# Loading attention rows in 32-row transfers, quarter by quarter from two queues, with a new merge order

## The chip, the cores and the metric

One core of a Trainium2 chip runs the whole program. The metric is the device time of one execution in microseconds (us); lower is better. The engines named here are TensorE (PE, with its weight loads PEld), VectorE (DVE), ScalarE (ACT), GpSimd (POOL) and SyncE (SP), which here only issues transfers. A transfer (DMA) is issued by SP or by ACT, in the order of that engine's own instructions, and is carried out by the core's 16 DMA engines.

## The reference

The input x has 8 batches of 512 tokens with 128 features. Stage A is a global attention, stage B two layers of a windowed attention with a gated MLP.

```python
h = layernorm(x) * (1 + ca) + sa
q = (h @ Wq + bq).reshape(b, 16, 8, 512)     # k, v alike: a reshape, no transpose
attn = softmax(einsum('bhdt,bhds->bhts', k, v) * temperature)
x = x + ga * einsum('bhdt,bhts->bhds', q, attn).reshape(b, t, d)
h = layernorm(x) * (1 + cb) + sb
y = h
for l in range(2):                            # windows of 64, 8 heads of 64
    y = layer(y)                              # shift, qkv, norms, rotary, attention, gated MLP
x = x + gb * y
```

The reshape matters here: one attention head is made of whole tokens. A head's 8 rows of 512 numbers are the 32 tokens' features laid end to end, so k and v have to be laid out anew, by way of DRAM, before the scores can be computed.

## The kernel before

**Stage A** works on one batch at a time, batches 0 to 7. k and v are each split into a high part and a low part (`hi`, `lo`), written to the DRAM scratch tensors `k_scr` and `v_scr` by four transfers each (`a_parts`, or `values_first` on ACT for batch 0), and read back as rows into `k_rows` and `v_rows`. The scratch has the shape (q, hh, 4, 8, 512), with head = 4q + hh. For one hh, "a quarter" below, the rows are 4 heads (q = 0 to 3) of 32 rows with 512 numbers: 128 partitions of 2 KB, 256 KB in all. `rows_in` reads such a quarter in the pieces that `PIECES` lists: for hh = 0 one transfer of 4 heads, for hh = 1 one of 3 heads and one of 1, for hh = 2 two of 2, for hh = 3 one of 1 and one of 3; seven transfers for k and seven for v. `v_rows` has two slots, `k_rows` one. SP issues all the v quarters of a batch (`a_values_in`), then the k quarters one by one (`a_keys_in`), where quarter hh of batch b waits until batch b-1 has finished its maxima for it. Only batch 0 is different: its k quarters come from SP and its v quarters from ACT (`values_first_in`), ahead of ACT's first work of the merged streams.

A batch has 32 steps n, 8 for each quarter. Step n is a pair of score matmuls on 32 partitions (`a_scores`, L436), a row maximum on DVE (L1151), two exponentials on ACT (L866); every second step the weights are normed by a reciprocal (L1155) and a product on POOL (L764), and the values are summed by 4 matmuls (`a_values`, L445) into one bank over the whole batch. The scores of a quarter wait for its v rows and k rows (`rows_landed`). At its end, DVE multiplies the sum by a gate (L1162) and POOL adds it to x (L753).

**Stage B** works in two streams, x with batches 0, 1, 2, 4, 6 and y with 3, 5, 7. Stream x starts while stage A is running; stream y has buffers that stage A also uses and begins when all of A is over. A batch of B enters with a layer norm (`b_enter_var`, `b_enter_normalize`), a transposition (L487) and a modulation on ACT (L921), and then has per layer 12 projections (L494), 8 transpositions (L501), windowed attention (L512 to L540), the output product (L550), the MLP (L569, L575), and at its end a transposition (`b_leave`) and two DVE operations (`b_out`, L1282 and L1286).

**The order** in which an engine takes steps of the three streams is written out by hand in `ORDER`: one letter for each step of stage A (`a`), stream x and stream y. Each engine has its own string and works through it in that order; semaphores hold it up where data isn't there. `BANKS` names the PSUM bank of every matmul step of PE's string. PE's string has 1166 letters, and both versions of a string have equally many of each letter, but for SP's.

Of the kernel before, what the change touches and what calls it, by code (L numbers as in the profile page):

```python
# [48 lines left out]
PIECES = [[(q, n, (q + hh) % HQ) for q, n in ((0, HQ - hh), (HQ - hh, hh)) if n] for hh in range(HQ)]  # L49
# [29 lines left out]
    ),
    "DVE": (  # L80
        "aaaaaaaaaaaaaaaaaaaaaaaaaaaaaaaaaaaaaaaaaaaaaaaaaaaaaaaaaaaaaaaaaaxaaaaaxaaaaaaaaaxaaaaaaaaaaxxaaaxx"
        "aaxxaxxaaxxaxaaxaaaaaaaaaaxaaaaaaaaaaaaxxaaxaaaaaaaaaaaaxxxaaaxaaxxxxaxaaaxxaaxxxaaaxxaaaaaaaxaaaxax"
        "aaaaxaxaaaaaaxaxaxaaaxxaaaaaxaaaxaaaxaxaaxaxaxaxxaaxaxaxaaaaaaaaaaaxaaaaxxaxxxxaaaxaaxxaaxxxaaaaxxxx"
        "axaaxaaxaaxaaxaxaaaaaaaxaxaaaaaaxxxaaaaxaaaaaaxaxaaaxaaaaaaxaaaaxaxxaxaaaxxxaaxxaaaxxaxaaaaaaaaaxaaa"
        "aaaaaaaaaaxxaxxxxaaaxxxaxxxaaaaaxxxxaxaaxaaaxaaxaaaaxaxaaaxaaaxaaaaaxxxaaaaxaxaaaxaaxaxaaxxaxxaaxxaa"
        "axaxxaaaaaaaaxaaaaaaxxxxaxxaxaaaaaxxxxxaaaxxaxxxaaaxaaaxaaaxaaxaxaaaxaxaaaaaaaxxxaaaxaaaaaaxxaxayxyx"
        "xxyxxxxxxxyxyxyyyyxyxxyxxyxxxyyyxxxxxxxxxxyxxyyxyyyyyxxyxyyyxyyyyyyyxxxxxyxyxyyyxyxxxxxyyxyxyxyxyyyx"
        "yxyxyxxxxyyxxxyyxyxxxyxxxxxxyyyxyyyyyxxyxyyyxyyyxxxyyyxyxxyyxyyxyxyxxxxxxxxyyyxyxyxyyxyxxxxyxxyxyxyx"
        "xxxyyyyxxxyyxyxxyxyyyxyyyyyxxyxyyyxyyyyyyxxxyxxyxyxyyyxyxxxxxyyxxyxyxyyyyxyxxyyxxxxyyxxxyyxxxyxxyxxx"
        "xxyyyxyyyyyxxyxyyyxyyyxxxyyyxyxxyyxyyxyxxxyxxxxxyyxxyxyxyyyxyxxxxxxyxyxxyxxxyxxyxxxyxyyyxxyyxyxxxyyy"  # L90
        "yyyyxxxyyyxxyyyyyyyyxyxxyxyxxyyyxyxxxxyyxyyyyxyyyyxxyxxxxyyxyyxxxxyxyxxxxxyxxyyxyyyyyxxyyyyyyxyyyyxy"
        "yyyyxxyxyxxyyyyy"
    ),
    "ACT": (
        "aaaaaaaaaaaaaaaaaaaaaaaaaaaaaaaaaaaaaaaaaaaaaaaaxaaaaaaaaxaaaaxaaaaxxxxaxxxxaaxxaxxaxaaxaxxxxaxaaaxx"
        "xaaaaaaaaaaaxxaaaaaaaaaxaaxxxaxxxaaaxxxaxxaxaaaxaaaaxaaaaxxaaaxaaaaaxaaaxaxxaxaxaxxxaxxaxaxaxaaxxxxa"
        "aaaxaaxxxaxaaaxxaaxxxaxaxaxxxaaaaxxxxaaaxxaaaxaaaaaxaxaaaxaaaaaaaaxaaaxxaaaaxxaxxxxxxaxxaxaxaaxaaaxx"
        "xaxxaaaaxxaxxaaaaaaaaxxaxaaxxxxxaxaxaaxxxaxaxxaaaaaxaaaaxaaaxaaxaaaxaxaxxxxaxaxxxaxxaxaxaaaxxxxxaaxa"
        "aaxxaaxaaxxxxxaaaxaxxxaaxxaxxaaxaxxaaaaxaaaxaxaaaxaaaaaaaxxxyxxxxxxyxyxxxxxyyyxyyyxxxxxyyyxxyxyxyxxy"
        "xxxxyyyxxyyxxyxyxxxyyxxyyyyxyyyyxyyxyyyxyxyyxxxyxxxyxxxyxxyxxyxxxxyyxyyxxxyyyxyyxxyyxxxxyxyxyyxxxyxy"  # L100
        "yxxyyyxyxyyyyxyyyxyyyxyxyyyyyxxyxxyxxxxxxxyxxxxyxxxxxxyxxxxyyxyxyyxyyxxxyyyxxyyxyxyyxxxyyyyxyxyyyyxy"
        "yyyxyyyxyyyxyxyyyxyyxxxyxxxyxxxyxxyxxxxxyxxyyxxyyyxxyyyyxxyyxxxxyxyxxyyyyxyxxyxxyyxyxyyyyxyyyyxyyxyx"
        "yyyyyxxyxxyxxxxxxxxyxxyxxxxxxxxxyxxyyxxyxyyxyxyxxyxyxxyxxyxxyyyxxyyyyxyyyyxyyxyyxyyyyyxyyyyxxyyxxyxx"
        "yyxxxyxxxyyxyxxxxxyxxxyyxyyyyyyyyxxyyxxxyxxxyyyyxyxxxyyxyxyxxyyyyyyyyxyyyyxyyxyyxyyyy"
    ),
# [1314 lines left out]
```

## Time and profile before

| | us |
|---|---|
| median of three runs | 1280.28 (1274.93 to 1286.37) |
| the profiled execution's own time | 1273.49 |
| its span, from the first to the last instruction | 1271.4 |
| PE busy / DVE busy / ACT busy / POOL busy in the span | 1046.8 / 946.8 / 922.3 / 504.1 |

The profiled execution is faster than the median run by 6.8 us. A row of the trace has a start, a duration, the engine, the line of the kernel, the operation and its tensors, and how often it came; in brackets how long the engine stood idle before it and what ended that. `SPq` and `ACTq` are these engines' issuing of transfers, and their durations are those of the issuing instructions, not of the transfers.

### The profile page before, as it was taken

Reading aid. Unit: us, or ns where it says so; the run is one execution under the profiler, and the core shown is the slowest. Engines: PE = TensorE matmul, PEld = TensorE weight load, DVE = VectorE, ACT = ScalarE, POOL = GpSimd, SP = SyncE. Lnnn points to the kernel's source line nnn. Section 1 sums busy time; section 2 is a strip of 40 time slices with the busy share of each in tenths; the row PEclk is TensorE's granted clock in tenths of the full one; section 3 lists DMA queues with packets and bytes.
Section 4 is the critical chain, followed back from the end, with each engine's and each line's share of the span. In section 5 each row is a group of like instructions: output and inputs, shape, how many; then the busy total and the mean of one; then the engine's idle time right before and its main releaser. Section 6 shows DMA issues by size and latency. Waiting matters only on the chain.

```text
span 1271.4 us, 23838 instructions
## 1 busy us (share of the span) xinstructions
PE 1046.8 (82%) x8124; PEld 524.9 (41%) x8124; DVE 946.8 (74%) x1945; ACT 922.3 (73%) x2782; POOL 504.1 (40%) x577
## 2 busy tenths in 40 slices
PE   2678888798888878988877898888898888898888
PEld 2232234333432334334324644644553553554463
DVE  2669977888779868776789578578758769758854
ACT  1688789788978897879855866756666765875673
POOL 4011523134312621343028437516735725645740
PEclk8687889897888888968888999999899999998999
DMA  6331213022021140210001101101100200110110
GB/s 209 138 132 36 101 43 106 28 67 82 16 97 45 34 117 13 88 58 19 1 9 30 31 1 30 31 10 38 30 2 1 47 23 9 31 30 1 31 31 17
DMA packets 24647, 59.15 MB, mean 47 GB/s; under 512 B 2832, under 2 KB 3024, under 8 KB 23376
## 3 DMA queue, kind: packets, MB, share of 16 engines
q1 hardware_dynamic: 23394, 55.53, 14.6%
q10 hardware_dynamic: 1134, 2.10, 0.5%
q8 instruction: 67, 1.10, 0.4%
q14 instruction: 52, 0.43, 0.1%
HBM read 23.98 MB, written 18.87 MB: 34 GB/s over the span
## 4 chain that ended last, share of the span: by engine, by line
PE 41%; DVE 30%; ACT 14%; issue 6%; POOL 4%; DMA 3%; SPq 1%; ACTq 0%; DVEq 0%; POOLq 0%
DVE neg_max L1151 8%; PE psum L494 6%; PE psum L445 5%; ACT E L866 5%; PE psum L550 4%; PE psum L569 4%; PE psum L436 4%; PE psum L540 4%; ACT rot_work L960 4%; DVE rot_work L1218 3%; DVE work L1214 3%; DVE ss L1222 3%; PE psum L575 3%; PE psum L529 2%; PE psum L519 2%
## 5 line engine op out<-in xcount | busy, mean ns | idle before, releaser
L866 ACT ACTIVATE E<-psum,neg_max 128x512 f32<-128x512 f32 x512 | 347.3, 704 | 85.0 <-DVE neg_max L1151 63.1
L1151 DVE TENSOR_REDUCE neg_max<-psum 128x2 f32<-128x1024 f32 x256 | 308.2, 1214 | 80.3 <-PE psum L436 78.0
L786 POOL TENSOR_TENSOR work<-work,rot_work 128x512 f32<-128x512 f32 x128 | 162.7, 1272 | 159.5 <-DVE rot_work L1218 159.2
L436 PE MATMUL psum<-v_rows,k_rows 32*128 32x512 f32 x512 | 135.0, 554 | 96.2 <-ACT E L866 56.7
L799 POOL TENSOR_TENSOR rot_work<-rot_work,rz 128x512 f32<-128x512 f32 x128 | 132.7, 1042 | 183.5 <-DVE rz L1245 183.4
L960 ACT ACTIVATE rot_work<-psum,neg 128x128 f32<-128x128 f32 x512 | 182.8, 394 | 29.9 <-DVE neg L1240 16.0
L494 PE MATMUL psum<-wqkv_sb,hs 128*128 128x512 f32 x384 | 188.7, 620 | 9.6 <-DVE hs L1208 4.3
L445 PE MATMUL psum<-E,qz 128*32 128x512 f32 x1024 | 160.8, 705 | 2.5 <-POOL qz L764 2.5
L764 POOL TENSOR_TENSOR qz<-qT,rz 128x32 f32<-128x32 f32 x128 | 31.0, 242 | 329.7 <-DVE rz L1155 317.1
L436 PEld LDWEIGHTS psum<-v_rows,k_rows 32*128 32x128 f32 x512 | 53.0, 205 | 247.9 <-issue 133.0
L794 POOL TENSOR_TENSOR work<-work,rn 128x512 f32<-128x512 f32 x128 | 133.0, 1052 | 28.7 <-DVE rn L1110 28.4
L960 ACT ACTIVATION_READ_ACCUMULATOR rot_work<-psum,neg 128x1 f32 x512 | 119.1, 233 | 0.0
L501 PE MATMUL psum<-ident,work 128*128 128x128 f32 x512 | 88.1, 307 | 33.4 <-POOL work L794 29.9
L866 ACT ACTIVATION_READ_ACCUMULATOR E<-psum,neg_max 128x1 f32 x512 | 113.2, 221 | 0.0
L932 ACT ACTIVATE rot_work<-psum 128x512 f32<-128x512 f32 x128 | 76.9, 605 | 46.7 <-DVE ss L1222 24.1
L1240 DVE TENSOR_REDUCE neg<-psum 128x4 f32<-128x512 f32 x128 | 85.4, 677 | 30.6 <-PE psum L519 30.3
L529 PE MATMUL psum<-ident,rot_work 128*128 128x128 f32 x512 | 83.6, 291 | 28.3 <-POOL rot_work L799 21.9
L494 PEld LDWEIGHTS psum<-wqkv_sb,hs 128*128 128x128 f32 x384 | 65.3, 191 | 91.6 <-issue 50.6
L569 PE MATMUL psum<-work,w_sb 128*128 128x512 f32 (+1 forms) x192 | 95.7, 634 | 5.2 <-ACT work L975 4.0
L1214 DVE TENSOR_TENSOR work<-psum,rot 128x512 f32<-128x512 f32 x128 | 87.0, 679 | 17.2 <-ACT rot_work L932 16.1
L970 ACT ACTIVATE prT<-psum 128x512 f32<-128x512 f32 x128 | 78.4, 620 | 25.0 <-PE psum L540 16.7
L501 PEld LDWEIGHTS psum<-ident,work 128*128 128x128 f32 x512 | 62.7, 155 | 71.5 <-POOL work L794 54.5
(121 smaller groups left out, 1679.3 us busy)
## 6 DMA issues: line engine op xcount, KB each, us to landing
work<-v_al SPq DMA_DIRECT2D x16, 512.0 KB, 4.4
work<-v_al SPq DMA_DIRECT2D x16, 384.0 KB, 6.2
k_scr<-hi SPq DMA_DIRECT2D x16, 256.0 KB, 3.0
k_scr<-lo SPq DMA_DIRECT2D x16, 256.0 KB, 3.4
v_scr<-hi SPq DMA_DIRECT2D x14, 256.0 KB, 3.1
v_scr<-lo SPq DMA_DIRECT2D x14, 256.0 KB, 3.4
k_rows<-k_scr SPq DMA_DIRECT2D x16, 192.0 KB
v_rows<-v_scr SPq DMA_DIRECT2D x14, 192.0 KB
```

The lines of the kernel that those rows point to most:

```text
L436: pe.matmul(bank, k_rows[r:r + 32, hh, P * j:P * (j + 1)], v_rows[r:r + 32, b % 2, hh, :], start=True, stop=True).then_inc(full, 1)
L445: last = pe.matmul(O_BANK[32 * q:32 * q + 32, :], qz[:, hh, j % QZ_SLOTS, q, :], E[:, (b * NG + g) % E_RING, q, :], start=(g == 0), stop=( ...
L494: pe.matmul(bank, hs[s][:, P * i:P * (i + 1)], wqkv_sb[:, l, INNER * c:INNER * (c + 1)], start=True, stop=True).then_inc(full, 1)
L501: last = pe.transpose(bank[:, P * p:P * (p + 1)], qk[s][:, i, w, P * p:P * (p + 1)], ident[:])
L569: pe.matmul(bank[0:CH[c]], w1_sb[:, l, o:o + CH[c]], h2T[s], start=True, stop=True).then_inc(full, 1)
L786: pool.tensor_tensor(qk[s][:, i, w, :], qk[s][:, i, w, :], sinp[s][:, n % 2, :], ALU.add).then_inc(rot_sum[s], 1)
L794: pool.tensor_tensor(v, v, rn[s][:, i, w, :].unsqueeze(2).broadcast_to([P, H, DH]), ALU.mult).then_inc((q_ready, k_ready)[w][s], 1)
L799: pool.tensor_tensor(pr[s][:, u % PR_SLOTS], pr[s][:, u % PR_SLOTS], rz2[s][:, u, :].unsqueeze(2).broadcast_to([P, 4, 2 * W]), ALU.mult).t ...
L866: act.activation(E[:, (b * NG + g) % E_RING, 2 * half + m, :], pair[:, m], ACT.Exp, bias=neg_max[:, n, m:m + 1], accum_out=z[:, n, m:m + 1 ...
L960: last = act.activation(pr[s][:, u % PR_SLOTS, w, :], bank[:, 2 * W * w:2 * W * (w + 1)], ACT.Exp, bias=neg2[s][:, u, w:w + 1], accum_out= ...
L1151: dve.tensor_reduce(neg_max[:, n, :], pair, AX.X, ALU.max, negate=True).then_inc(max_ready, 1)
L1214: dve.tensor_tensor(qk[s][:, i, w, :].rearrange("p (h d) -> p h d", h=H), bank.rearrange("p (h d) -> p h d", h=H), rot[:, l, i, w, 0, :].u ...
```

## The change

`PIECES` is gone. `rows_in` now issues four transfers of 32 rows (64 KB) for each quarter, one per head, to the same places as before. For k and v together a batch has 32 row transfers instead of 14. In batch 0, ACT issues only the v rows of quarter 0; SP issues the k rows of quarter 0, then v and k of quarter 1, of 2 and of 3. In the later batches SP still issues all v quarters ahead of the k quarters, but each v quarter is a step of its own in the merge order.

```diff
-PIECES = [[(q, n, (q + hh) % HQ) for q, n in ((0, HQ - hh), (HQ - hh, hh)) if n] for hh in range(HQ)]
+def group_of(q, hh):
+    return (q + hh) % HQ
...
         def rows_landed(eng, s, b, hh):
-            passed(eng, s[hh], 16 * len(PIECES[hh]) * (b + 1))
+            passed(eng, s[hh], 16 * HQ * (b + 1))
 
         def rows_in(eng, dst, scr, hh, landed):
-            for q, m, r in PIECES[hh]:
-                eng.dma_start(dst[32 * r:32 * (r + m)].bitcast(F32),
-                              scr[q:q + m, hh].rearrange("q t d s -> q (t d) s")).then_inc(landed[hh], 16)
+            for q in range(HQ):
+                r = 32 * group_of(q, hh)
+                eng.dma_start(dst[r:r + 32].bitcast(F32), scr[q, hh].rearrange("t d s -> (t d) s")).then_inc(landed[hh], 16)
...
-            def a_values_in(b):
+            def a_values_in(b, hh):
                 passed(sp, v_out, (b + 1) * 16 * 4)
-                for hh in range(HQ):
-                    rows_in(sp, v_rows[:, b % 2, hh], v_scr, hh, v_in)
+                rows_in(sp, v_rows[:, b % 2, hh], v_scr, hh, v_in)
...
-                    a_values_in(b)
-                    yield
+                    for hh in range(HQ):
+                        a_values_in(b, hh)
+                        yield
                     for hh in range(HQ):
                         a_keys_in(b, hh)
                         yield
...
             a_parts(0, 0)
             for hh in range(HQ):
+                if hh:
+                    a_values_in(0, hh)
                 a_keys_in(0, hh)
...
             def values_first_in():
                 passed(act, v_out, 16 * 4)
-                for hh in range(HQ):
-                    rows_in(act, v_rows[:, 0, hh], v_scr, hh, v_in)
+                rows_in(act, v_rows[:, 0, 0], v_scr, 0, v_in)
```

All five strings of `ORDER`, and `BANKS`, are new. Counted out letter by letter:

- PE's first 93 letters, DVE's 71, ACT's 71 and POOL's 33 are as before, so batch 0 of stage A and the first half of batch 1 are in the old order.
- Stream x runs 10 steps of PE behind its old place where batch 5 of stage A begins (84 steps done, 94 before), and is level again where batch 7 begins (161 and 161).
- SP takes the store of stream x's first batch ahead of batch 6's scratch writes (it was ahead of the last k quarter of batch 5), and the shifted value copies of x's second batch (`b_shift_v`, L684 and L685) after batch 6's third k quarter (they stood between its k writes and its v writes).
- The hand-over from stage A to stream y differs. PE's string around it is shown below; the last `a` in each line is the last value sum of batch 7. Before, x's `b_leave` and the DVE work of `b_out` and `b_enter_var` for the next batch came before the end of A, and six projections of x before y's first transposition. After, `b_leave` follows A's last step, DVE takes A's last gate product, then `b_out`, the variances of both streams, and the two normalizations; y's first transposition comes straight after x's, then two projections of x, then twelve steps of y.
- In stage B stream x led by about 17 steps of PE and y's last batch ended last; now y leads by about 16 and x's last batch ends last. The last letters are a mirror image: the one stream's eight last MLP steps alone.

```diff
 # PE, letters 601 to 700
-        "aaxxxxxxxyxxxxxxyyyyyyyxxyxxyyyxyxxxxxyxyxxxyxyxxyxxyxyyxxxyxyxyyyxyyyyxyyxxxxyyxxxyyxxyxyxxyxxxxxxx"
+        "axxyxxyyyyyyyyyyyyxxxxyxxyxxyxxyyyyyyyxxyxyyyyxxyyxyyxyxyyyxyxyxxxyxxxxyxyxyyyyyxxyxxyyxyxyyxyyyyyyy"
 # SP
-        "aaaaaaaaaaaaaaxaaaaaaaaaaaaaaxaaaaaaxaaxaaaaaaaaaaaaaxxxyxyxyxyxyxyxyxyxy"
+        "aaaaaaaaaaaaaaaaaaaaxaaaaaaaaaaaaaaaaaaaaxaaaaaaaaaaxaaaaaaaaaxaaaaaaaaaaaxxyxyxyxyxyxyxyxyxyx"
...
```

## Rows read from the trace of the kernel before

**Rows 1.** The page: busy tenths of 40 slices, granted TensorE clock, DMA share.
```profile
PE   2678888798888878988877898888898888898888
DVE  2669977888779868776789578578758769758854
ACT  1688789788978897879855866756666765875673
PEclk8687889897888888968888999999899999998999
DMA  6331213022021140210001101101100200110110
```
**Rows 2.** The timeline of the start: start us, us, engine, line, operation, count [idle before].
```profile
22.69 0.84 ACTq L872 DMA_DIRECT2D v_scr<-hi  x1
24.32 8.15 SPq L362 DMA_DIRECT2D k_rows<-k_scr  x7
27.64 12.64 ACTq L362 DMA_DIRECT2D v_rows<-v_scr  x7
37.40 1.22 PE L436 MATMUL psum<-v_rows,k_rows 32*128 32x512 f32 x6 [20.12 <-DMA v_rows<-v_scr]
38.27 2.36 DVE L1151 TENSOR_REDUCE neg_max<-psum 128x2 f32<-128x1024 f32 x2 [16.20 <-PE psum L436]
40.38 0.69 ACT L866 ACTIVATE E<-psum,neg_max 128x512 f32<-128x512 f32 x1 [25.78 <-DVE neg_max L1151]
```
**Rows 3.** The DMA queues' view: kilobytes each and median us from issue to landing.
```profile
k_scr<-lo SPq DMA_DIRECT2D x16, 256.0 KB, 3.4
cols<-in_cols SPq DMA_DIRECT2D x1, 14.0 KB, 1.9
```
**Rows 4.** Windows, SP: window, length, TensorE clock, DMA share, GB/s.
```profile
63.90:66.40 2.50, 1.00 0.87 270
75.00:81.00 6.00, 1.00 0.25 77
150.00:160.00 10.00, 0.53 0.15 57
46.00:48.00 2.00, 0.50 0.13 51
```
**Rows 5.** The chain of waits, 200 to 225 us: batch 3's first six v row issues, singly.
```profile
207.51 0.60 SPq L362
...
208.16 0.74 SPq L362
...
208.95 0.46 SPq L362
...
209.46 0.59 SPq L362
...
210.66 1.76 SPq L362
```
**Rows 6.** Timeline, 74 to 98 us, where batch 1 begins.
```profile
75.05 5.57 SPq L362 DMA_DIRECT2D v_rows<-v_scr  x7
80.73 13.10 SPq L362 DMA_DIRECT2D k_rows<-k_scr  x7
88.93 0.79 PE L436 MATMUL psum<-v_rows,k_rows 32*128 32x512 f32 x2
94.32 0.79 PE L436 MATMUL psum<-v_rows,k_rows 32*128 32x512 f32 x2 [4.59 <-issue]
95.15 1.23 DVE L1151 TENSOR_REDUCE neg_max<-psum 128x2 f32<-128x1024 f32 x1 [4.04 <-PE psum L436]
97.12 0.69 ACT L866 ACTIVATE E<-psum,neg_max 128x512 f32<-128x512 f32 x1 [4.56 <-PE psum L445]
```
**Rows 7.** The chain of waits, 440 to 480 us, where batch 6 begins.
```profile
447.47 2.17 SPq L656
...
454.00 0.61 SPq L362
...
459.88 14.31 DMA k_rows<-k_scr
...
474.28 0.50 PE psum L436 x2
```
**Rows 8.** Timeline of the PE queue, 455 to 476 us.
```profile
474.28 0.50 PE L436 MATMUL psum<-v_rows,k_rows 32*128 32x512 f32 x2 [2.98 <-DMA k_rows<-k_scr]
```
**Rows 9.** Timeline of the hand-over, 640 to 660 us.
```profile
642.22 0.86 DVE L1099 BATCH_NORM_STATS2 stats<-x_sb 128x6 f32<-128x128 f32 x4
644.23 1.06 PE L445 MATMUL psum<-E,qz 128*32 128x512 f32 x8 [1.78 <-POOL qz L764]
644.28 0.16 DVE L1108 SCALAR_TENSOR_TENSOR tmp<-var,rstd 128x4 f32<-128x4 f32 x1 [0.43 <-ACT rstd L914]
645.90 0.68 DVE L1162 TENSOR_TENSOR kf<-psum,gate_bc 128x512 f32<-128x512 f32 x1
650.59 8.10 PE L494 MATMUL psum<-wqkv_sb,hs 128*128 128x512 f32 x12 [3.43 <-DVE hs L1208]
658.97 5.41 PE L494 MATMUL psum<-wqkv_sb,hs 128*128 128x512 f32 x12
```
**Rows 10.** Windows, all engines: length, busy us (count) of PE PEld DVE ACT POOL, clock.
```profile
37.40:646.70 609.30, 506.96 (x3317) 210.12 (x3318) 488.60 (x890) 503.34 (x1488) 171.80 (x260) 0.86 0.20 63
646.70:1271.40 624.70, 530.55 (x4775) 307.30 (x4773) 448.96 (x1023) 415.56 (x1288) 318.37 (x289) 0.96 0.09 21
```

More of the change, by code:

```diff
@@ L82 @@
[L82 to L86, printed above, removed]
@@ L92 @@
-        "yyyyxxyxyxxyyyyy"
+        "aaaaaaaaaaaaaaaaaaaaaaaaaaaaaaaaaaaaaaaaaaaaaaaaaaaaaaaaaaaaaaaaaaxaaaaxaaaaaaaaaxaaaaaaaaaaxaxxaaax"
+        "xaaxxaxaaaxxaaaxxaaaaaaaaaaaaaaaxaaaaaaaaaaaaaaaaaaaaaaaaaxxaaxaxxxaxaaaxxaaxxxaaaaxxxxaxaaxaaaaxaaa"
+        "aaxaaaaaxaxaxaaxaaaaaaaxxxaaxaxaaaaxaxaaxaxaaaaxxxaxxaaaxxaaaxaaaaaaaaaxaaaaaaaaaaaaaaaaaaaaaxxaxxxx"
+        "aaaxaaaaxaaaxxxaxaaxxxxaaaxxaaaxaaaaaxaxaaxaaxaaaxaaaaaaaaxaaxxaxaaaxaaxaaaaxaaaaxaaaaaaxxxaxaaaxxxa"
+        "axxaxaaxxaaaaxaaxxaxxxxaaxxxxxxxxaaxaxxaaxaxaaaaxaaaaaxaxaxaaxaaaaaaxxaxaaxaxaaaaxaaxaxaaaxaaaxxxaax"
@@ new lines @@
+        "xaxxaaaxaaaaaxaaaaaaaaxxaaaxxxxaxaaaaxxaxxxaaaaaxxaxxxaaaxxaaaxaaxaxaaaaaxaaxaaaaaaaaxxxaaaxaxxyxyxy"
+        "xyyyyyyyyyyxyxyxxxxyxyyxyyxyyyxxyyyyyyyyyyxyyxxyxxxxxyyxyxxxyxxxxxxyyyxyyxyxyxxxyxyyyyyxxyyxyxyxxxxx"
+        "xxyyyxxyyyyxyxyxyxyyyyyyyyyyxxxyxxxxxyyxyxxxyxxxxxxyyyxyxyxyyxxxyxyyyyyyyyxxxyyxyxyxxyxyyyxyyyxxyyyx"
+        "xxxyyyxyyxyyyxyxxyxxxyxxxxxyyxyxxxyxxxyxxxyyxyyxyxyxxxyxyyyyyxxxyyxyxyxyxyyyyxxyyxxxxyyyxxxyyyxyyyyy"
+        "yyxyxxxyyxxxyxxxyxxxxxyyyxxxyxyxyxyxxyxyyyyxyyyyyxxxyyxyxxxyxyyyyxyyxyxxxxyyxxyyyxxyyxyyyxyyxxxyxxxx"
@@ L93 @@
+        "xyyxyxxxyxxxyyyxxxxyyxyxyxxxyxyyyyyxxxyyxyxyxxxxxxxxxxyxyyxyyyyxyxxyxxyxxyyyxxxyyyyxxxyxyxyxxxyxyyxy"
+        "xyxxxyyyxyyxxxxx"
     ),
     "ACT": (
[L95 to L98, printed above, removed]
@@ L104 @@
[L104 removed]
+        "aaaaaaaaaaaaaaaaaaaaaaaaaaaaaaaaaaaaaaaaaaaaaaaaxaaaaaaaaxaaaaxaaaaxxxxxxaxxxaaxxaxaxaaaaxxxxxaaxaaa"
+        "aaxxxaaaaaaaaaaaaaaaaaaaxxaaxxxaaaxxxaxaxaaxxxaxaaxaxaaaaaaxaaaxaaxaaaxaaxaaxxaxxaxxaxxxaxaaxxaxaaxx"
+        "xaaxxaaaaaxxxxaaaaaaaaaaaaaaaxxaxaxaxaxaxaaxxaxaxxxaxaaaxxaaaaxaaaxaaaxaaxaaaaaaaaxaaaxaxaaxaxxxaxxx"
+        "xxaxaaxxaxaaxxxxxaxaxxxaaxxxxxxaaxxxxxaxaxxaxxaaaaaaxaaaxaaxaaaxaaxaaxxaxxaxxaxxaaxxaaxxaxaxxxxaaxaa"
@@ new lines @@
+        "axxxxaaaaaxaxaxaaxxaxxaxxxaaaxaxxxaxaxaaaxaaaaxaaxaaaaxaaxyxxyyxxyyyyyyyyyyyyxxxyxxyyyyxxyyxxyyxyxyy"
+        "yyyxyxxxyyxyyyyxxyyxxyyxxxxyxxxxyxxyxxyxxyxxyyyxyyyxyyyxyyxyyyyyyyxxxxxxxxxxyyyyxxyyxxyyyyyxxxyyyyyx"
+        "xyyxxxyxyxxxxyxxxyxxxyxxyxxxxyxyyxyyxyyyyyyyyyyxyyyyyyxyyyxyxyxyxxxyxxyyxyyxxxxyxyyxyyyyxxxyxxxxxxyx"
+        "xxxyxxxxyxxyxyxxxyxxyyyxyyyxyyyxyyxyyxyyyyxyxyyyyxxyxxxyyxxxyxyyxxyyxxyyxyyxxyyxxyxyxxxyxxxyxxxxyxxy"
+        "xxxxxyyxyyxyyyyyyyyyyxyxyyyyyyyxyyyxxyxyxxxyxxyxyxxyxxxyyxyyyxyxyyxxxxyxxxyxxxxyxxxxyxxyxyxxxyxxyyyx"
@@ L434, in a_scores @@
                 for m, (bank, full) in enumerate(pair):
-                    r = 32 * ((2 * half + m + hh) % HQ)
+                    r = 32 * group_of(2 * half + m, hh)
                     pe.matmul(bank, k_rows[r:r + 32, hh, P * j:P * (j + 1)], v_rows[r:r + 32, b % 2, hh, :],
```

68 lines of the change are left out of this document (29 added, 39 removed).

## The prediction

> **What bounds the kernel now.** I read the page's slices first [rows 1]. After the start no engine is idle for long and none is full: PE, DVE and ACT take turns. Split at the end of stage A [rows 10], A's 609.3 us have DVE busy for 488.6, PE for 507.0 (at a mean clock of 0.86) and ACT for 503.3, so A is a chain through three nearly equal engines, where a wait in one goes to the end unless the next has slack. Stage B's 624.7 us have PE busy for 530.6: PE leads there, and nothing of the change touches its work. What stands out against this is the start. PE is idle for 20.1 us until 37.40, released by v rows, and ACT's first exponential starts at 40.38 [rows 2].
>
> Then the transfers. Scratch writes fill the 16 DMA engines (share 0.87, 270 GB/s). Row reads don't: 0.25 and 77 GB/s while the v rows of batch 1 are read, 0.15 later, 0.13 at the end of batch 0's [rows 4]. These shares are about 4, 2.4 and 2 of 16 engines, and the transfers there cover 4, 3 or 2 heads each. So I take it that a row transfer uses as many engines as its heads, and that bytes are not the limit: rows of one head alone are the open point. By the Trainium skill, DMA: Bandwidth & Descriptors, section "Why a DMA increments its semaphore by 16 and not by 1", a transfer runs on the largest number of engines up to 16 that divides the slowest dimension of both sides; a one-head transfer would use 16. By that rule the trace agrees for 4 and 2 heads, and no row isolates one head.
>
> **The sum, part by part**, against the profiled execution's 1273.49 us.
>
> *Start.* The v scratch has landed at 27.64. Before, ACT then issues seven v transfers for 12.64 us, while SP still has k transfers under way, and quarter 0 is complete at 37.40 [rows 2]. After, ACT issues four of 32 rows. The nearest row for one is the third issue of batch 3's v rows, which has 32 rows and took 0.46 us; ACT's own issue of a scratch write took 0.84 [rows 2, 5]. I take 0.7: the last starts 2.1 us after the first. To landing I take 2.5 us, between the 1.9 of a small load and the 3.4 of a 256 KB write [rows 3]. That gives 27.64 + 2.1 + 2.5 = 32.3 for the first score, 5.1 us earlier. SP's quarter 1 of v goes out at the same time, 256 KB beside 256 KB, which at 270 GB/s [rows 4] together take 1.9 us and are inside the 2.5. Ends: 27.64 + 1.4 + 1.9 = 30.9, and 27.64 + 2.5 + 3.4 = 33.5 or, for the transfers in each other's way, 34.4; a gain of 6.5 to 3.0. Also, ACT is not free until 27.64 + 12.64 = 40.28, though the first maximum, half of the pair of 2.36 from 38.27, is there at 39.5 [rows 2]: another 0.9. **Start: -6.0 us (-7.4 to -3.0).** What is late next is only PE at half clock. DVE, ACT and POOL follow in the same order, because the orders of batch 0 are unchanged.
>
> *Batch 1.* PE stands still for 4.59 us between the last scores of batch 0 and the first of batch 1; DVE then idles 4.04 and ACT 4.56 [rows 6]. The profile calls it "issue", but the step that follows is the first to need k quarter 0, and that quarter's issue began at 80.73 only, behind the 1 MB of v, read at 77 GB/s. After, 16 v issues come first and then 4 of k. At 0.50 us each with the gap (0.46 and 0.04) that is 10.0 us, and 75.05 + 10.0 + 2.5 = 87.6, ahead of 89.7 where PE became ready. Both ends of this shift with the start. The stall goes as long as an issue costs less than (89.7 - 75.05 - 2.5) / 20 = 0.61 us. **-4.0 us (-4.6 to 0)**, DVE's idle time.
>
> *Batch 6.* PE waits 2.98 us for k quarter 0, issued at 459.88 and landed 14.31 later [rows 7, 8]. Its v scratch writes were held up too: one took 2.17 us to issue, because x's two shift copies had gone out just ahead, and the new SP order puts those behind. By the same count k would land at 454.00 + 12.5 = 466.5. ACT and DVE had stream x's work to do meanwhile, so I take two thirds: **-2 us (-3.9 to 0)**; the far end adds a second v row wait of 0.9. In the other batches k is read a good part of a batch ahead, and its speed is worth nothing; what hides it is the remaining steps of the batch before.
>
> *Hand-over.* Here the new order costs. Before, A's last value sum ends at 644.23 + 1.06 = 645.3, x's output and variance are done by then (from 642.22) and its normalization is under way, and PE gets the first projection at 650.59: 5.3 us [rows 9]. After, DVE has in turn the gate product (0.68), x's output (two operations, 1.3 us, from `b_out`'s work of the same size as that product), x's variance (642.22 to 644.28, with the log less 0.5: 1.6), y's variance and two memsets (1.9), and x's normalization (644.28 to 645.90, 1.6): 7.1 us. Then come transposition, modulation and shift: 650.59 - 645.90 = 4.7 before, in which DVE also did the gate product and y's variance ahead of the shift; I take 3.5 for the three alone. That is 10.6 instead of 5.3. From these 5.3 I take 1.0 off, because A's own last steps get rid of DVE's work ahead of them and y's first projections come earlier. The idle time also keeps the clock low: six projections took 8.10 us after this idle stretch and 5.41 at the higher level [rows 9], and up to 2.7 us more lies there. **+4.3 us (0 to +7).**
>
> *The rest of the order.* Each engine has the same steps in number, kind and size. A has the same work of x interleaved at its end, B's streams swap the lead, and the last eight steps are mirrored. I find no row that prices a reordering, so I take 0 and allow 6 us either way, 0.5% of the span. SP's 18 further issues per batch cost SP 9 us; what hides them is SP's waiting, since it issues nothing that PE needs for most of a batch. If that cover were gone, batch 1 is where it shows, as above.
>
> Sum: -6.0 - 4.0 - 2.0 + 4.3 = -7.7, so 1265.8 us for an execution like the profiled one. The median run stood 6.8 us above it; scaled to 1280.28, the forecast is 1280.28 x 1265.8 / 1273.49 = 1272.5 us, 0.6% faster.
>
> **Rivals.**
>
> *More gain.* The hand-over costs nothing, because y's projections fill it, and all three waits go fully: -7.4 - 4.6 - 3.9 = -15.9, or 1264 us. For it: in stage A three engines are close, so shorter waits come through. Against: B has PE busy for only 85% of its time [rows 10], yet idle PE time at a stage's head can't be made up from that. Chance 0.34.
>
> *The read isn't faster* (the change doesn't do what it says): 32 rows still move at 77 GB/s, the source side being the limit. Then only the order of the start helps: k quarter 0, then v quarters 0 and 1 together, 512 KB in 6.8 us, so 27.64 + 6.8 = 34.4, a gain of 3.0 and 0.9; batch 1's k lands as late as before. -3.9 + 4.3 = +0.4, or 1281 us. Against it stand the shares, which fall with the heads per transfer [rows 4]. Chance 0.10.
>
> *Issuing becomes the bound* (slower). Place: SP's row of 20 issues between the v scratch's landing and k quarter 0. The sixth issue in batch 3, 32 rows as well, took 1.76 us [rows 5]. At that price k lands 20 x 1.80 + 2.5 = 38.5 us after 75.05, at 113.6, and PE waits 24 us in batch 1 instead of 4.6. The start gains nothing (four issues, 7.2 us, and 2.5), and with the hand-over the kernel is at +24, 1304 us. It decides from 0.61 us an issue on, and outweighs all gains at about 1.0 us. Against: that issue came behind five transfers on few engines, and the same shape with an empty queue took 0.46. Chance 0.12, of which half for a price near 1 us. A page rule points the same way: the Trainium skill, DMA: Bandwidth & Descriptors, "Rules for kernel authors", says to coalesce small transfers, as under 64 KB mostly overhead is paid. By that rule these 64 KB pieces are at the edge; the trace speaks for the split so far, since a 256 KB quarter on 4 engines ran at 77 GB/s [rows 4].
>
> **Numbers.** Forecast 0.44, more gain 0.34, no faster read 0.10, issue-bound 0.12. The cases' bounds reach from 1280 - 16 - 6 = 1258 to 1281 + 6 = 1287; with the runs' own scatter I give 1256 to 1287. A measurement of this kernel tells about 1% from no change. The forecast case lies at 0.6% with its spread, so a fifth of it is over 1%; of more gain (1.2%) two thirds: 0.34 faster. Slower by over 1% (above 1293): half of the issue-bound case and a part of a bad new order, 0.12. Within 1%: 0.54.
>
> **What would show it.** PE's first scores at about 32 us and the first exponential at about 34; a DMA share near 0.8 in row reads instead of 0.25; issues of 32 rows at about 0.5 us; no idle PE between batch 0's last and batch 1's first scores; no wait on k rows where batch 6 begins; and some 10 us, not 5.3, from A's last value sum to the first projection. The prediction is wrong if 32-row issues cost over 0.6 us, if the hand-over costs nothing, or if stage B's time between hand-over and end moves by more than 6 us.

## The result, and the profile after

The changed kernel is slower: 1285.59 us (median of 20 runs, 1283.0 to 1290.93) against 1278.2 us (20 runs of the kernel before beside them). The ratio is 1.0053, with a 95% interval of 1.0037 to 1.0069. That is inside the forecast's range and inside 1%, but on the other side of no change than the forecast of 0.6% faster. That the range holds it is luck: its upper end of 1287 came from the rival in which the read isn't faster, and that is not what happened. The profiled execution took 1283.0 us, with a span of 1281.0 against 1271.4 before.

The page of the changed kernel, busy tenths of 40 slices, TensorE clock and DMA share, to be read beside [rows 1]:

```profile
PE   2778887898888878988877898888898788889797
DVE  2878986888767958886788578577758768857845
ACT  1888689877977788879846856756765765785594
PEclk8788689997988879969988999998998999999899
DMA  6532223041220410410001101101100010110110
```

No slice stands out, as a loss of 10 us over 1280 would not. What stands out is what got better. The start, from the timeline of 20 to 42 us, against [rows 2]:

```profile
27.57 1.70 SPq L366 DMA_DIRECT2D v_rows<-v_scr  x4
27.58 1.78 ACTq L366 DMA_DIRECT2D v_rows<-v_scr  x4
31.70 1.22 PE L439 MATMUL psum<-v_rows,k_rows 32*128 32x512 f32 x6 [14.42 <-DMA v_rows<-v_scr]
32.56 2.36 DVE L1155 TENSOR_REDUCE neg_max<-psum 128x2 f32<-128x1024 f32 x2 [10.51 <-PE psum L439]
33.88 0.69 ACT L871 ACTIVATE E<-psum,neg_max 128x512 f32<-128x512 f32 x1 [19.29 <-DVE neg_max L1155]
```

Four issues now take 1.78 us where seven took 12.64, and the first scores come 5.7 us earlier, the first exponential 6.5. The DMA view, against [rows 3], and the windows (length, busy us and count of PE, PEld, DVE, ACT and POOL, clock, DMA share, GB/s), against [rows 4, 10]:

```profile
k_rows<-k_scr SPq DMA_DIRECT2D x128, 64.0 KB, 1.9
v_rows<-v_scr SPq DMA_DIRECT2D x124, 64.0 KB, 1.9
```
```profile
20.00:40.00 20.00, 3.60 (x12) 1.45 (x12) 9.29 (x22) 5.15 (x17) 7.51 (x14) 0.53 0.75 214
37.00:647.00 610.00, 512.29 (x3306) 210.97 (x3306) 485.13 (x874) 499.71 (x1480) 172.97 (x260) 0.86 0.22 62
642.40:1277.20 634.80, 538.55 (x4780) 316.25 (x4780) 453.40 (x1042) 418.24 (x1290) 317.99 (x289) 0.95 0.09 21
```

In these 20 us the share is 0.75 where it was 0.49 before, but they hold scratch writes too. Row reads alone stand in these two windows, the first with both queues issuing, the second with SP alone (v rows of batch 1):

```profile
29.00:31.70 2.70, 0.00 (x0) 0.00 (x0) 0.00 (x0) 0.00 (x0) 0.00 (x0) 0.50 0.81 220
71.00:77.00 6.00, 4.63 (x36) 2.08 (x32) 3.78 (x6) 5.58 (x17) 0.24 (x1) 1.00 0.41 114
```

The first has a share of 0.81 and 220 GB/s, where the kernel before had 0.33 and 119 in the same stretch. The second has 0.41 and 114 GB/s, against 0.25 and 77 in [rows 4]. So with one queue issuing, the gain is 1.5 times and not 3 times. That is about SP's own pace of issuing: 16 issues in 8.79 us are 0.55 us for 64 KB, or 119 GB/s. A 64 KB piece issued by SP lands 1.9 us after its issue by the median; the four of ACT at the start took 2.3. Where batch 1 begins (timeline, 76 to 92 us) PE no longer stands still for k rows, as it did in [rows 6]:

```profile
78.76 9.26 SPq L366 DMA_DIRECT2D k_rows<-k_scr  x16
84.21 1.64 PE L439 MATMUL psum<-v_rows,k_rows 32*128 32x512 f32 x4
87.64 1.13 PE L439 MATMUL psum<-v_rows,k_rows 32*128 32x512 f32 x4
```

The wait of batch 6 [rows 8] is gone too. What got worse is the hand-over (timeline, 636 to 665 us), against [rows 9]:

```profile
640.45 1.92 PE L448 MATMUL psum<-E,qz 128*32 128x512 f32 x16
642.44 0.69 DVE L1166 TENSOR_TENSOR kf<-psum,gate_bc 128x512 f32<-128x512 f32 x1 [1.13 <-PE psum L448]
643.09 0.69 DVE L1286 TENSOR_TENSOR prT<-psum,gate_bc 128x512 f32<-128x512 f32 x1
644.94 0.86 DVE L1103 BATCH_NORM_STATS2 stats<-x_sb 128x6 f32<-128x128 f32 x4
646.90 0.87 DVE L1103 BATCH_NORM_STATS2 stats<-x_sb 128x6 f32<-128x128 f32 x4
648.96 1.12 DVE L1118 TENSOR_SCALAR rot_work<-x_sb,mv,rstd 128x128 f32<-128x128 f32 x4
650.13 1.12 PE L490 MATMUL psum<-ident,rot_work 128*128 128x128 f32 x4 [7.09 <-DVE rot_work L1118]
653.33 11.98 PE L497 MATMUL psum<-wqkv_sb,hs 128*128 128x512 f32 x23 [0.44 <-ACT hs L930]
```

From the end of A's last value sum (640.45 + 1.92 = 642.4) to the first projection (653.3) are 11.0 us, where 5.3 were before. PE is idle for 7.09 of them, until DVE has done the gate product, x's output, both variances and x's normalization.

To find the rest I followed the same steps of DVE through the two traces (start in us; the last column is e1 below, the new transfers in the old order):

| step | before | after | e1 |
|---|---|---|---|
| first maximum of batch 0 | 38.3 | 32.6 | 32.3 |
| of batch 1 | 95.1 | 86.3 | 86.2 |
| of batch 4 | 313.0 | 303.2 | 309.0 |
| of batch 5 | 393.8 | 377.1 | 389.7 |
| of batch 6 | 474.8 | 479.1 | 468.9 |
| of batch 7 | 564.4 | 562.9 | 556.8 |
| A's last gate product | 645.9 | 642.4 | 637.4 |
| last output of B | 1267.5 | 1277.2 | 1258.1 |

The lead grows to 16.7 us by batch 5 and is gone at batch 6. Between the last two rows lie 621.6 us before, 634.8 after, 620.7 in e1. So the loss has two places: stage A around batches 4 to 6, and stage B with its hand-over (+13.2 us; 5.6 of them lie ahead of the leading stream's first shifted value copy, which SP issues 38.1 us after the gate product before and 43.7 after). One profiled execution is not exact. Stage A of the same program came 4.2 us apart in two of them (after and e10). Stage B in the old order with the old hand-over took 620.7 to 625.0 us in five (before, e1, e6, e8, e9), and the longer ones had more time at the low clock: 37.5 us in e1, 61.3 in e9. Verdicts below go by the medians, and traces are used where several agree.

### The profile page after: what moved, and what is told of

Same layout as the page of the kernel before. It is cut to its first block, busy times and chain, and to the rows that moved or that the text cites. A ratio compares the mean times of both kernels' runs of the same rounds, so it can differ in the third digit from the quotient of the medians.

```text
span 1281.0 us, 23984 instructions
## 1 busy us (share of the span) xinstructions
PE 1061.6 (83%) x8124; PEld 535.3 (42%) x8124; DVE 948.9 (74%) x1945; ACT 923.7 (72%) x2782; POOL 503.6 (39%) x577
## 4 chain that ended last, share of the span: by engine, by line
PE 29%; DVE 19%; ACT 8%; POOL 4%; issue 4%; ACTq 0%; DVEq 0%; POOLq 0%
PE psum L497 4%; PE psum L572 4%; PE psum L543 4%; PE psum L553 4%; DVE work L1218 3%; DVE rot_work L1222 3%; PE psum L532 2%; ACT rot_work L964 2%; DVE ss L1226 2%; PE psum L522 2%; PE psum L578 2%; POOL rot_work L804 2%; PE psum L448 2%; DVE neg_max L1155 2%; POOL work L799 1%
## 5 line engine op out<-in xcount | busy, mean ns | idle before, releaser
L497 PE MATMUL psum<-wqkv_sb,hs 128*128 128x512 f32 x384 | 190.4, 632 | 10.6 <-DVE hs L1212 6.0
L448 PE MATMUL psum<-E,qz 128*32 128x512 f32 x1024 | 164.4, 721 | 0.0
L504 PE MATMUL psum<-ident,work 128*128 128x128 f32 x512 | 91.8, 319 | 31.9 <-POOL work L799 26.0
L497 PEld LDWEIGHTS psum<-wqkv_sb,hs 128*128 128x128 f32 x384 | 68.8, 197 | 99.1 <-issue 60.2
L504 PEld LDWEIGHTS psum<-ident,work 128*128 128x128 f32 x512 | 65.7, 161 | 76.1 <-POOL work L799 53.9
```

The source lines that it names most:

```text
L448: last = pe.matmul(O_BANK[32 * q:32 * q + 32, :], qz[:, hh, j % QZ_SLOTS, q, :], E[:, (b * NG + g) % E_RING, q, :], start=(g == 0), stop=( ...
L497: pe.matmul(bank, hs[s][:, P * i:P * (i + 1)], wqkv_sb[:, l, INNER * c:INNER * (c + 1)], start=True, stop=True).then_inc(full, 1)
L504: last = pe.transpose(bank[:, P * p:P * (p + 1)], qk[s][:, i, w, P * p:P * (p + 1)], ident[:])
```

## The experiments

Theory O: the transfers and the new start pay about what the forecast gave them, and the new order costs more. Its rival: the transfers cost something later on. Theory C: the order costs by way of the clock, idle PE time lowering it. All ratios are to the kernel before on the same chip, with 95% intervals. Where an edit is a splice of the written-out orders, the diff names the parts; `BANKS` always goes with PE's string.

**e1, the transfers alone.**

```diff
 # against the kernel after
-ORDER, BANKS: new
+ORDER, BANKS: as before (SP's a_values_in in its four steps, one behind the other)
```

> The changed kernel's transfers and start with the merge order and banks of before (the four v quarters are one step of SP again). Theory O (the transfers gain what was forecast and the new order gives it away): the start's -6 us and batch 1's -3 us reach the end, ratio to before 0.990 to 0.993, stage A's last gate product some 10 us earlier than 645.9. Rival T (stage A or B takes the gain back whatever the order, because a later bound holds): ratio 0.998 to 1.004, with the gain gone before batch 7.

1264.85 us, ratio 0.9877 [0.9853, 0.9901]: 1.2% faster than before, 15 us in the medians (1280.09 beside it), which is more than was expected. The rival falls. No version in the study is measurably faster (e12, at 1263.64 us, is e1 with unneeded work), and it beats both the kernel before and the changed one.

**e2, the order alone.**

```diff
 # against the kernel after
+PIECES = [[(q, n, (q + hh) % HQ) for q, n in ((0, HQ - hh), (HQ - hh, hh)) if n] for hh in range(HQ)]
...
-                rows_in(act, v_rows[:, 0, 0], v_scr, 0, v_in)
+                for hh in range(HQ): rows_in(act, v_rows[:, 0, hh], v_scr, hh, v_in)
```

> The new merge order and banks with the transfers and start of before (PIECES). Theory O: the order alone costs about 1.3 to 1.5%, ratio 1.012 to 1.016. Rival T: the order alone costs at most 0.5%, ratio 0.998 to 1.005.

1295.18 us, ratio 1.0117 [1.0090, 1.0144]: the order costs 1.2% by itself. With the new transfers under it, it costs 1.0053 / 0.9877 = 1.8%, some 22 us. The two parts are thus not additive: under the new order the transfers give back only half of what they give under the old one.

**e3 and e4, half of the order each**, cut at the hand-over, with the new transfers.

```diff
 # e3, against the kernel after
-stage B: new
+stage B: old
 # e4, against the kernel after
-stage A: new
+stage A: old (x's normalization ahead of A's end)
```

> The changed kernel with the new order up to stage A's end and the order of before from there on (x's variance and normalization for its third batch directly behind x's output on DVE). The trace after has A's end 3.5 us earlier and the kernel's end 9.6 later, so B lost 13. Theory O with the loss in B's order: ratio 0.996 to 0.999. Rival: B's time is set by something other than its order, ratio 1.004 to 1.008 as for the whole change.

> The changed kernel with the order of before up to stage A's end (with x's early variance and normalization) and the new order from there on. Theory O: A's end 10 to 12 us earlier than before, B some 8 to 13 us longer, ratio 0.999 to 1.003. Rival T: as the whole change, 1.005.

e3: 1279.53 us, 1.0001 [0.9980, 1.0021]; e4: 1273.98 us, 0.9946 [0.9927, 0.9965]. Against e1 the new A with its hand-over costs 1.3%, the new B 0.7%, together about the 1.8% of the whole. Both halves cost. e3 came out above what was expected and e4 below: the loss was looked for in B, and the new B is the smaller part.

**e5, the hand-over alone**, on e1: DVE takes x's output, variance and normalization behind A's last gate product.

```diff
 # DVE, around the last a
-"...xxxaaaxaaaaaaxxaxayxyx"
+"...xxxaaaxaaaaaaaaxxyxxyx"
```

> The kernel of e1 with one change in DVE's order, where stage A ends: x's output and x's variance and normalization come behind A's last gate product, as in the new order, and y's variance ahead of x's normalization. Theory O: the hand-over costs the forecast 4 to 5 us, ratio to before 0.991 to 0.993 (e1: 0.988), x's first projection some 10 us after A's last value sum. Rival: stage B makes the gap up again, ratio as e1 within 0.1%.

1271.28 us, 0.9940 [0.9921, 0.9959], so 6.4 us above e1. The two hand-overs, first e1's timeline of 630 to 655 us, then e5's of 630 to 662:

```profile
635.74 1.06 PE L448 MATMUL psum<-E,qz 128*32 128x512 f32 x8 [1.79 <-POOL qz L769]
636.39 1.11 DVE L1118 TENSOR_SCALAR rot_work<-x_sb,mv,rstd 128x128 f32<-128x128 f32 x4
637.42 0.68 DVE L1166 TENSOR_TENSOR kf<-psum,gate_bc 128x512 f32<-128x512 f32 x1
642.10 7.00 PE L497 MATMUL psum<-wqkv_sb,hs 128*128 128x512 f32 x12 [3.89 <-DVE hs L1212]
```
```profile
632.80 1.07 PE L448 MATMUL psum<-E,qz 128*32 128x512 f32 x8 [1.07 <-POOL qz L769]
633.93 0.69 DVE L1166 TENSOR_TENSOR kf<-psum,gate_bc 128x512 f32<-128x512 f32 x1 [1.51 <-PE psum L448]
641.62 1.11 PE L490 MATMUL psum<-ident,rot_work 128*128 128x128 f32 x4 [7.75 <-DVE rot_work L1118]
644.79 7.23 PE L497 MATMUL psum<-wqkv_sb,hs 128*128 128x512 f32 x12 [2.06 <-ACT hs L930]
```

In e1 the normalization runs while PE still sums A's values, and the first projection starts 642.10 - 636.80 = 5.3 us after the last sum. In e5 it is 644.79 - 633.87 = 10.9 us. e5's stage A ends 3.5 us earlier, but not for this edit: e5 is already 3.6 us ahead at batch 5's first maximum (386.1 against 389.7), where the two programs are still the same. What the edit costs is read behind A's end. From the last gate product to the leading stream's first output in B are 191.7 us in e1 and 197.9 in e5, 6.2 more; the medians say 6.4. The same stretch takes 191.9 to 193.0 us in the other executions with the old B and the early normalization (before, e6, e8, e9, e12), and 196.9 to 197.9 in those with the late one (e3, e7, e11).

**e6, the order around batches 4 to 6 alone**: PE's steps 278 to 455 and the same stretch of the other engines; all else as e1.

```diff
 # PE, letters 301 to 400
-"axaaaaxxxaaaxaxaaaaaxaaaaaaaaaxaxxxxxaxaaaxaaaaxaaaaaaaaaaxaaaaxxxxxxaxaaxxxxaaaxaxaaaaxxaaxaaaaaaax"
+"aaaxaaxaaaaxaxaaxaxaaxxxaxaaaaaxxxaaaaxaaxaaaaxaaaaaaxaxxxaxaxxaaxaaxaaaaaaaaaaaaxaaaaaxaxxxxxxaaxxx"
```

> The kernel of e1 with the new order (all engines and banks) only in a window of stage A, from x's attention in layer 1 of its first batch to the output product of layer 0 of its second (PE's steps 278 to 455; both orders have done the same steps at both ends), where the new order first lets A run ahead by 17 us and x fall behind. Theory O: this window costs some 9 to 10 us, ratio to before 0.994 to 0.997. Rival: the order's loss is spread evenly over A and B, then this window costs at most 3 us, ratio 0.988 to 0.990.

1277.57 us, 1.0001 [0.9978, 1.0025]: 12.7 us above e1 in the medians, more than was expected. The window in e1 and in e6 (columns as above):

```profile
309.00:490.30 181.30, 152.68 (x1204) 67.73 (x1198) 148.21 (x285) 154.21 (x484) 54.38 (x78) 0.91 0.22 60
```
```profile
306.70:504.50 197.80, 160.07 (x1191) 70.61 (x1188) 149.27 (x285) 156.00 (x487) 54.76 (x79) 0.85 0.20 55
```

The same steps take 16.5 us more. This holds in every trace: from batch 4's first maximum to batch 6's are 159.5 to 162.0 us in the eight executions with the old order there, and 176.0 to 177.7 in the five with the new one (after, e2, e3, e6, e10). PE is busy for 7.4 us more at a clock of 0.85 instead of 0.91, and idle for 37.7 instead of 28.6. It spends 58.0 us at the low clock instead of 34.1. No transfer is among the waits that grew. The waits in the two windows (us in total, times, longest), e1 first:

```profile
DVE neg_max L1155 <- PE psum L439: 13.8, 20, 5.4
PE psum L439 <- ACT E L871: 12.2, 16, 1.8
...
ACT E L871 <- DVE neg_max L1155: 10.8, 13, 2.3
```
```profile
PE psum L439 <- ACT E L871: 23.7, 22, 3.2
ACT E L871 <- DVE neg_max L1155: 20.3, 17, 3.5
DVE neg_max L1155 <- PE psum L439: 18.4, 21, 2.4
```

All three links of stage A's own round grow: scores wait for exponentials, exponentials for maxima, maxima for scores. My reading, which no run isolates, is that an engine does this when it has only one stream's work in its string. In the new order A's steps come first for a while and stream x drops behind: its first output comes at 407.1 us instead of 389.3 (409.6 in e6, 385.3 in e1). Then x's steps have to be made up in a dense block while A waits. Between the middle of batch 5 and batch 6's first maximum lie 60.0 us in the changed kernel, against 36.8 before; most of these 23 us are x's work moved there (PE is idle for 10.2 of them against 9.7), and what is lost over the window is the 16. Which engine's string does the harm was not tried: strings and banks hang together. Nor was the clock in this window: no run fills PE's idle time in stage A, so theory C stays open there.

**e7, the rest of the new A**: new up to PE's step 277 and from 456 to the end of A, with the late hand-over; the old order in between and in B.

```diff
 # against e1
-stage A outside the window of e6, hand-over: old
+stage A outside the window of e6, hand-over: new
```

> The complement in stage A: new order up to that window and from it to A's end (with x's variance and normalization directly behind x's output), the old order in the window and in stage B. Theory O: A outside the window gains 3 to 5 us in the new order and the late hand-over takes them back, ratio to before 0.986 to 0.990. Rival (loss spread evenly): ratio 0.993 or more.

1273.53 us, 0.9956 [0.9938, 0.9974]: 0.8% above e1, where e5's hand-over makes 0.6%. That misses the expectation (0.986 to 0.990) and lies in its rival's range: outside the window, A gained nothing here to set against the hand-over. The window of e6 is still the dearest part of A. The parts of A (1.3% in e6, 0.8% in e7) sum to more than the whole of it in e3 (1.3%), so a splice costs something at its seams, and the medians' 12.7 us of e6 is an upper bound. The traces show both halves of this. In e7 the window itself, in the old order, took 167.7 us instead of 160. And from batch 6's first maximum to batch 7's, the whole new A (after, e2, e3, e10) takes 83.7 to 83.8 us where the old takes 87.7 or more, a gain of 4 us that neither splice keeps (88.2 and 88.7).

**e8 and e9, the start taken apart.** e8 is e1 with all 16 v pieces of batch 0 on ACT and all k pieces on SP. e9 is the kernel before with only the new distribution over the queues, and its seven large transfers.

```diff
 # e8, against e1
-                rows_in(act, v_rows[:, 0, 0], v_scr, 0, v_in)
+                for hh in range(HQ):
+                    rows_in(act, v_rows[:, 0, hh], v_scr, hh, v_in)
 # e9, against the kernel before
-                for hh in range(HQ):
-                    rows_in(act, v_rows[:, 0, hh], v_scr, hh, v_in)
+                rows_in(act, v_rows[:, 0, 0], v_scr, 0, v_in)
...
+                if hh:
+                    passed(sp, v_out, 16 * 4)
+                    rows_in(sp, v_rows[:, 0, hh], v_scr, hh, v_in)
                 a_keys_in(0, hh)
```

> The kernel of e1 with batch 0's rows issued as before: ACT issues all 16 v transfers of 32 rows, SP all 16 of k. At 0.45 us an issue ACT is busy with them to 27.6 + 7.2 = 34.8, the first scores come at about 31.7 as in e1, and the first exponential is 1 us later than e1's 33.9. Theory (the faster reads give the start, not who issues): ratio within 0.1 to 0.2% of e1's 0.988. Rival (the quarter by quarter order gives it): first scores at 34 or later, ratio 0.990 to 0.993.

> The kernel of before, with its seven transfers and its order, and only the start's new distribution: ACT reads v quarter 0, SP the k quarter 0, then v and k of quarters 1 to 3. v quarter 0 still moves on 4 heads' worth of engines. Theory (engines per transfer decide): first scores at 27.6 + 256 KB at 77 GB/s (3.4) + the k and v beside it, some 34 to 35 instead of 37.4, ratio 0.994 to 0.998, batch 1's stall of 4.6 us still there. Rival (the order of issue alone gives the start): first scores at 32, ratio 0.990 to 0.993.

e8: 1267.76 us, 0.9923 [0.9898, 0.9947]; e9: 1277.46 us, 0.9983 [0.9955, 1.0011]. The start of e8, then the start of e9, then e9 where batch 1 begins:

```profile
27.54 7.46 ACTq L366 DMA_DIRECT2D v_rows<-v_scr  x16
32.05 1.22 PE L439 MATMUL psum<-v_rows,k_rows 32*128 32x512 f32 x6 [14.91 <-DMA v_rows<-v_scr]
35.10 0.69 ACT L869 ACTIVATE E<-psum,neg_max 128x512 f32<-128x512 f32 x1 [20.52 <-DVE neg_max L1154]
```
```profile
27.28 1.10 ACTq L362 DMA_DIRECT2D v_rows<-v_scr  x1
35.11 1.22 PE L436 MATMUL psum<-v_rows,k_rows 32*128 32x512 f32 x6 [17.84 <-DMA v_rows<-v_scr]
37.29 0.69 ACT L869 ACTIVATE E<-psum,neg_max 128x512 f32<-128x512 f32 x1 [22.71 <-DVE neg_max L1153]
```
```profile
78.07 13.66 SPq L362 DMA_DIRECT2D k_rows<-k_scr  x7
91.59 0.79 PE L436 MATMUL psum<-v_rows,k_rows 32*128 32x512 f32 x2 [5.98 <-DMA k_rows<-k_scr]
```

The piece size does most of it. e1 and e9 differ in the size alone: 1264.85 against 1277.46 us, 1.1%, and e9 by itself is not clear of no change. With small pieces the scores start at 32.05 whichever queue issues them, with one large piece, alone at the head of ACT's queue, not before 35.11. The distribution frees ACT 1.2 us earlier (33.88 in the changed kernel, 35.10 in e8). But e8's ratio was expected within 0.2% of e1's and lies 0.5% above it, in the rival's range: the medians give the distribution 2.9 us, with intervals that just overlap, and the trace shows 1.2 of them. And with large pieces the stall of batch 1 is back, 5.98 us, whose releaser is now named as k rows.

**e10, the clock in the new B**: the changed kernel with short transpositions of an identity into 15 idle stretches of PE in B, 57 of them at the hand-over. This work is not needed for anything. It goes into a PSUM bank that PE now takes before it waits for its data. **e12** is the same on e1, at 14 places.

```diff
+            def fill(bank, *step):
+                for _ in range(FILL.get(step, 0)):
+                    pe.transpose(bank[:, 0:P], ident[:], ident[:])
```

> The changed kernel with work that nobody needs (transpositions of the identity, into the bank that PE has just taken and then overwrites) put into 15 of PE's idle gaps of stage B, 8 to 17 of them each and 57 at the hand-over. Theory C (idle gaps let the TensorE clock fall, and that is where stage B's time went): low-clock time in B falls from 68.5 us to 35 to 50, and the time by 4 to 9 us, ratio 0.998 to 1.002. Rival (the clock is a by-product): the added work delays PE, ratio 1.005 to 1.009.

> The kernel of e1 (new transfers, old order) with the same unneeded work in 14 of its own idle gaps of stage B. It has 40 us of low clock in B. Theory C: low-clock time falls to 15 to 30 us, ratio 0.982 to 0.986. Rival: ratio 0.988 to 0.992.

e10: 1283.57 us, 1.0025 [1.0002, 1.0048]; e12: 1263.64 us, 0.9876 [0.9839, 0.9914], e1 having 0.9877. Stage B in e1, e10 and e12, from A's last gate product to the last output (the changed kernel's is above):

```profile
637.40:1258.10 620.70, 529.38 (x4776) 307.48 (x4776) 449.33 (x1024) 415.20 (x1288) 318.01 (x289) 0.97 0.09 21
```
```profile
646.60:1275.30 628.70, 543.05 (x5004) 328.15 (x5004) 453.26 (x1041) 418.04 (x1290) 317.82 (x289) 0.99 0.09 21
```
```profile
633.00:1252.40 619.40, 537.56 (x4978) 320.20 (x4975) 447.82 (x1023) 414.66 (x1288) 318.08 (x289) 1.00 0.09 21
```

Over these windows TensorE is at the low level for 68.3 us after, 37.5 in e1, 13.7 in e10 and 5.5 in e12. The filler gives the changed kernel's B 6.1 us back (634.8 to 628.7), 2 us in the medians, which is hardly more than their scatter. It gives e1 nothing measurable. Low-clock time fell further than was expected in both, and neither ratio reached the range that C gave, nor did e10's reach the rival's. e12's interval still overlaps C's range at its lower end, and added work can itself delay PE, so a small share of the clock is not excluded. But C is at best a part of the loss in B: with hardly any low clock left in either, the new B at 628.7 us is still 9.3 behind the old one at 619.4.

**e11, does the lead matter?** e5 with the letters x and y exchanged in all of B: y leads, in the old rhythm.

```diff
 # against e5, stage B of every string
-x, y
+y, x
```

> The kernel of e5 with the letters of streams x and y exchanged in every string behind stage A's end: y leads and x follows, in the old interleaving. Theory (which stream leads is worth nothing, the interleaving's details are): ratio as e5's 0.994 within 0.2%. Rival (y in the lead is what costs B its time, for instance because stream y's buffers come free late): ratio 0.998 or more.

1269.82 us, 0.9919 [0.9890, 0.9949], as e5. Which stream leads is free. What B's new order costs beyond the hand-over (0.7% in e4, whose hand-over took 8.0 us, 2.7 more than e1's) lies in its interleaving. The traces put it into the middle: from the first to the second output of the leading stream 204.7 us before and 211.5 after, against 225.7 and 224.7 from there to the last output. The middle takes 204.8 to 206.2 us in all ten traces with the old B, 211.5 to 212.8 in the three with the new one (after, e2, e4), and 209.4 in e10, with the filler.

## Why the forecast was wrong

**Bounds.** The reading of stage A as a chain through three near-equal engines fits what e6 shows, and it was a reason to distrust the step that failed. "Nothing of the change touches its work", of stage B, was true of the steps and not of their order, and B lost 13.2 us.

**Start**, forecast -6.0: right. First scores 5.7 us earlier (5.1 forecast), first exponential 6.5 earlier. Issues took 0.45 us each (1.78 for four), where I took 0.7, and ACT's four landed in 2.3 by the median, where I took 2.5. The share of 0.81 with both queues issuing is the "near 0.8" of the forecast's signs; with SP alone it is 0.41, which the forecast did not foresee.

**Batch 1**, forecast -4.0: right in mechanism. PE's stall is gone, and the gain at batch 1's first maximum is 8.8 us against 5.7 at batch 0's. That is 3.1 more; in e4, e5, e6, e11 and e12, whose transfers and orders are the same up to there, the maximum comes at 83.5 to 84.5 instead of 86.3.

**Batch 6**, forecast -2: right. The wait is gone in e1 and after. From the middle of batch 5 to batch 6's first maximum are 36.9 us before and 37.2 in e9, both with large pieces, and 34.5 to 35.5 in e1, e4, e5, e8, e11 and e12 with small ones in the same order: some 2 us.

**The transfers together**, forecast -12: -9.4 in the profiled executions (e1's span of 1262.0 against 1271.4), -15 in the medians. The point left open, what a transfer of one head does, is settled by the trace: it is not held to few engines, since the share reaches 0.81 where reads over 2 to 4 heads ran at 0.25, 0.20 (35 to 38 us) and 0.13. The Trainium skill, DMA: Bandwidth & Descriptors, "Why a DMA increments its semaphore by 16 and not by 1", has a transfer spread over the largest number of engines up to 16 that divides the slowest dimension of both sides; by that rule the shares agree, being close to 4, 3 and 2 sixteenths and far above them for one head, though no stretch isolates 3 heads. The same page of the Trainium skill, in "Rules for kernel authors", would coalesce small transfers; here e1 and e9 show the other sign, since coalescing over heads takes the engines away, as the row "Use all 16 engines" of the same table says of an outermost dimension below 16. The prediction named the first row and not this one.

**Issuing as the bound**: the rival with 0.12 failed. Sixteen issues of 32 rows take 7.46 us at e8's start and 9.26 where batch 1 begins, with all gaps and waits: 0.47 to 0.58 each, below the 0.61 from which it decides. The slower result came from elsewhere.

**Hand-over**, forecast +4.3: right in mechanism, too small in size. From the last value sum to the first projection are 11.0 us (10.6 forecast). I had taken 1.0 us off the term for what y would make good; nothing was made good, and e5 measures 6.4 us, inside the term's range.

**The rest of the order** is the step that failed: "I find no row that prices a reordering, so I take 0 and allow 6 us either way, 0.5% of the span." The order costs 1.8% over e1, some 22 us, of which the hand-over is 6.4; 0 stood where about 15 belong. In medians the sum is thus -15 for the transfers and +22 for the order, +7, where the forecast had -12 and +4.3. With the old transfers (e2) the order costs 1.2%, which leaves about 9 us for this term; it is above the 6 that were allowed either way. What the runs show in its place is the window around batches 4 to 6 (16 us in five traces, partly given back behind it) and the middle of B (7 us). Looking back, two things were at hand to see it, though no run tests them as causes. Stage A's round over PE, DVE and ACT is nearly full [rows 10], so each engine needs the other stream's work as filling for each of its waits, and the count in the change said that x falls 10 steps behind by batch 5 and is level by batch 7: this is a dense block of x. And the order before may fit its stretch to within a few us, so that the two sides of a reordering are not alike: there is more room to lose than to gain. "Allow 6 us either way" had neither. "Stage B's time between hand-over and end moves by more than 6 us" was named as what would make the prediction wrong; it moved by 13.2, 5.6 of it the hand-over. The chances have a small slip too: a fifth of 0.44 and two thirds of 0.34 are 0.31 for faster by over 1%, not 0.34, and the 0.54 for within 1% was right with the wrong sign inside it.

Open: which engine's string costs in the window of e6, how much of its 7.4 us of longer PE work, at the lower clock, is cause and how much follows from the idle time, and what in the middle of B costs its 7 us. The clock's share was tested for B only, and came out as 2 us in the medians and 6 in the traces.

## What to carry over

Here reads over 2 to 4 heads ran at DMA shares of 0.13 to 0.25, and reads of one head each at up to 0.81. Split such a 256 KB read into 64 KB pieces when the wait for it is on the path, compare the DMA share over stretches that hold the same kind of transfer, and remember that one issuing queue alone came to 0.41. When a change brings its gain and a new hand-written order in one, price the order as a risk to one side, stretch by stage: the place where one stream falls behind and has to be made up, and the place where an engine takes a chain of steps that used to lie beside other work. Time the parts alone, since here one of them was worth -1.2% and the other +1.2% (+1.8% on top of the first), and the first alone was the better kernel.

## What the runs showed of the hardware

A 256 KB read over 4 heads in one transfer, with SP issuing quarter 1 beside it, needed 7.8 us to the first scores (27.28 to 35.11), and four of 64 KB, with the same beside them, needed 4.1 (27.58 to 31.70). Issuing the large ones was dear as well, 12.64 us for seven on ACT [rows 2] against 7.46 for sixteen (e8). One queue issued a 64 KB read every 0.45 to 0.58 us, so SP alone moved 114 GB/s and both queues together 220.

PE's granted clock fell to its 1.2 GHz level behind idle stretches of about 2 us in B (a gap of 2.3 us at 691.9, with the clock at 0.50 from 693.7 on, and of 2.2 at 848.8, at 0.50 from 850.7 on, in the changed kernel). Filling them lifts the clock from 0.97 to 1.00 in e12 without gaining time: B took 619.4 us instead of 620.7. Five executions of the same stage B took 620.7 to 625.0 us with 37.5 to 61.3 us at the low level, the longest with the most, so a part of the time may still be the clock's. In B, a low clock next to idle time was mostly a sign of a wait, not its cost.
